# Eight-expert feed-forward block: 39 tiles of 256 rows, or 25 tiles of 256 and 21 units of 128

## The chip, the core and the metric

The kernel runs on one core of a Trainium2 chip. What is measured is the device time of one execution in microseconds (us). The core has five engines with a queue each: TensorE (PE), which loads weights (PEld) and multiplies them with moving columns into PSUM; VectorE (DVE), ScalarE (ACT), GpSimd (POOL) and SyncE (SP). They wait for each other by semaphores.

## What is computed

4096 tokens of 256 channels pass a quaternion rotation, a linear layer, and a top-2-of-8 mixture of experts; then an output layer and the residual. The experts take most of the time.

```python
h = cond(x) @ W_in + b_in                       # x: 8 x 512 tokens, 256 channels
probs = softmax(h @ W_gate + b_gate)
topv, topi = top_k(probs, 2); topv /= sum(topv)
route = zeros_like(probs).at[rows, topi].set(topv)
mid = relu(einsum('nd,edh->neh', h, W1) + b1)    # W1: 8 experts, 256 x 1024
eout = einsum('neh,ehd->ned', mid, W2) + b2      # W2: 8 experts, 1024 x 256
out = x + einsum('ne,ned->nd', route, eout) @ W_out + b_out
```

Only the two chosen experts of a token are computed: 8192 rows in all, sorted by expert.

## The kernel before

**Front part.** x is turned and multiplied, the gate's logits are taken, `z` (the rows that the experts read) is stored to `zbuf` in 16 stores, and VectorE counts the rows of each expert, ranks the experts by count (`order_i`), and gives each row a slot. An expert's rows are padded to a multiple of TS = 256, so NTILE = (8192 + 8*255) // 256 = 39 tiles hold them whatever the counts. Slots become two index tables (`src`, `dst`) through one-hot matrices (L907, L910, L913) and matmuls (L1105). `tile_e` holds each tile's rank.

**Tiles.** Each number is held as a high and a low f16 part, so a product takes three matmuls. Tile a passes through these stages:

- POOL gathers 2 x 128 rows (`gather`, L514), SP turns them with a transposing DMA into `xs` (`turn`, L387).
- PE, first layer (`first_layer`, L1199 to L1201): 4 blocks b of 2 output groups c, each 2 x 3 matmuls of 256 columns: 48 matmuls. The weights lie at `w1_at(e, ...)`, an address made from the rank in a register, so the sequencer does a register operation ("ISA" in the order, FUSED_REGOPS in the trace) for two of three.
- ACT (`tile`, L654): bias, scale and relu of each block into `midf`, two operations of 256 columns.
- DVE (`tile`, L981 and L983): splits each block of 512 columns into high and low f16 (`mids`).
- PE, second layer (`second_layer`, L1229): 48 matmuls of 256 columns. It runs for tile a - 1 after the first layer of tile a.
- DVE (`y_out`, L971) scales the result and adds b2; POOL scatters it to `ybuf` (`scatter`, L522).

**Weights.** An expert's W1 and W2 arrive in f32 (`raw1`, `raw2`, one buffer each; SP, `load_w1` L371, `load_w2` L377), are squared and summed (ACT, L591 and L596; PE, `norms`) and split into f16 parts (ACT and DVE, `piece`; L603 and L793) while the tiles of the rank before run. GT = 4 tiles belong to each rank: phase 0 squares, phase 1 splits W1, phase 2 splits W2, and phase 3 does nothing. PE waits at a rank's first tile for `s_wl`, the count of split pieces. PE's tiles 4 to 27 are a hardware loop; the others are written out.

**End.** The last tile's second layer is done half by half (`last_rows`, L1215); then the pairs of results are loaded, mixed and projected, and the residual (loaded by `load_residual`, bias added in `add_bias`, two per tile from tile 30 on, L998) is added.

## Time and profile before

| | us |
|---|---|
| median of 3 runs (lowest, highest) | 553.31 (551.42, 557.58) |
| time of the profiled execution | 553.89 |
| its span in the trace | 552.1 |
| PE busy | 520.3 (94%) |
| DVE busy | 348.9 (63%) |
| ACT busy | 282.4 (51%) |
| POOL busy | 221.8 (40%) |

The span goes from the first to the last instruction. A matmul's duration in the trace holds its way through the array, which overlaps the next ones; the distance from start to start is what a stream of them costs.

### The profile page before, as it was taken

How to read it: one execution, taken by the hardware profiler on the slowest of the kernel's cores; microseconds unless marked ns; L12 is line 12 of the kernel's file. 1: busy time of each engine (PE TensorE's matmuls, PEld its weight loads, DVE VectorE, ACT ScalarE, POOL GpSimd, SP SyncE). 2: the span in 40 equal slices, each digit the busy share in tenths (PEclk: the TensorE clock that was granted, in tenths of full speed). 3: DMA queues.
4: the chain of work that ended last, by engine and by line, in shares of the span. 5: the costliest groups of instructions: out<-in, count | busy, mean ns of one | idle time of the engine just before them, and what ended most of it. 6: DMA issues, size and time to landing. Idle time of an engine off the chain costs nothing.

```text
span 552.1 us, 13863 instructions
## 1 busy us (share of the span) xinstructions
PE 520.3 (94%) x4337; PEld 450.1 (82%) x4338; DVE 348.9 (63%) x697; ACT 282.4 (51%) x499; POOL 221.8 (40%) x286
## 2 busy tenths in 40 slices
PE   7888966999999999999999999999999999994897
PEld 6555744888888888888888888888888888883786
DVE  4669896686675675665666666675556656651564
ACT  2335782766565565565654654754334324320662
POOL 4400007146373374374375365365334334212132
PEclk8798996999999999999999999999999999998799
DMA  7405445548465364255255256222445445304973
GB/s 210 145 2 165 169 134 161 146 136 171 79 153 162 76 186 128 67 160 163 69 142 170 76 149 166 69 74 78 116 118 143 124 115 137 76 20 142 387 291 134
DMA packets 82312, 74.68 MB, mean 135 GB/s; under 512 B 47511, under 2 KB 70236, under 8 KB 82268
## 3 DMA queue, kind: packets, MB, share of 16 engines
q1 hardware_dynamic: 72336, 49.96, 32.3%
q0 software_dynamic: 8608, 24.13, 14.2%
q8 instruction: 23, 0.38, 0.3%
q10 hardware_dynamic: 1324, 0.05, 0.2%
q14 instruction: 21, 0.17, 0.1%
HBM read 45.53 MB, written 18.61 MB: 116 GB/s over the span
## 4 chain that ended last, share of the span: by engine, by line
PE 85%; DVE 5%; DMA 5%; issue 1%; ACT 1%; SPq 1%; POOL 0%; POOLq 0%; DVEq 0%; ACTq 0%
PE bank L1229 36%; PE bank L1199 13%; PE bank L1200 12%; PE bank L1201 12%; PE bank L1267 5%; DMA z_by_token<-w1s 2%; DVE w1s L822 2%; PE bank L1277 1%; DMA w1s<-y_by_choice 1%; PE bank L1064 1%; DMA w1s<-in_x 1%; PE bank L1215 1%; PE bank L1094 1%; PE bank L1074 1%; DMA region<-z_by_token,src 1%
## 5 line engine op out<-in xcount | busy, mean ns | idle before, releaser
L654 ACT ACTIVATE region<-bank,b1p,cbits 128x256 f32<-128x256 f32 x312 | 159.1, 560 | 183.6 <-PE bank L1201 175.9
L1229 PE MATMUL bank<-w2s,region 128*128 x1824 | 205.3, 273 | 0.1
L1229 PEld LDWEIGHTS bank<-w2s,region 128*128 128x128 f16 x1824 | 178.4, 98 | 21.0 <-issue 0.4
L1199 PE MATMUL bank<-region,w1s 128*128 128x256 f16 x624 | 171.1, 274 | 0.9 <-ACT region L641 0.9
L1200 PE MATMUL bank<-region,w1s 128*128 128x256 f16 x624 | 171.1, 274 | 0.0
L1201 PE MATMUL bank<-region,w1s 128*128 128x256 f16 x624 | 171.0, 274 | 0.0
L522 POOL DMA_INDIRECT y_by_choice<-region,dst x78 | 84.5, 1083 | 189.7 <-DVE region L971 173.2
L514 POOL DMA_INDIRECT region<-z_by_token,src x78 | 77.5, 994 | 86.2 <-DMA z_by_token<-w1s 62.6
L983 DVE TENSOR_TENSOR region<-region 128x512 f16<-128x512 f32 x156 | 108.4, 695 | 5.4
L981 DVE CAST region<-region 128x512 f16<-128x512 f32 x156 | 67.7, 434 | 66.3 <-ACT region L654 61.2
L971 DVE SCALAR_TENSOR_TENSOR region<-bank,cbits,b2b 128x256 f32<-128x256 f32 x76 | 33.3, 479 | 78.4 <-PE bank L1229 77.9
L1199 PEld LDWEIGHTS bank<-region,w1s 128*128 x624 | 62.0, 99 | 8.7 <-issue 1.2
L1201 PEld LDWEIGHTS bank<-region,w1s 128*128 x624 | 61.4, 98 | 7.4
L1200 PEld LDWEIGHTS bank<-region,w1s 128*128 x624 | 61.4, 98 | 7.3
L1094 PE MATMUL bank<-w1s,w2s 128*128 128x256 f32 x128 | 33.3, 404 | 0.0
L1267 PE MATMUL bank<-wout,w2s 128*128 128x256 f32 x120 | 29.9, 394 | 0.0
L1094 PEld LDWEIGHTS bank<-w1s,w2s 128*128 128x128 f32 x128 | 23.8, 196 | 6.6 <-issue 3.8
L1267 PEld LDWEIGHTS bank<-wout,w2s 128*128 128x128 f32 x120 | 22.8, 200 | 2.7
L684 ACT ACTIVATE w2s<-w1s,route 128x256 f32<-128x256 f32 x28 | 12.7, 498 | 18.7 <-DMA w1s<-y_by_choice 18.6
L1277 PE MATMUL bank<-ident,w2s 128*128 128x128 f32 x64 | 10.8, 294 | 10.2 <-DVE w2s L1033 10.2
L603 ACT ACTIVATE w1s<-region,s 128x1024 f16<-128x1024 f32 x16 | 17.6, 1141 | 5.3 <-DVE s L786 5.3
L793 DVE SCALAR_TENSOR_TENSOR w2s<-region,s,w2s 128x1024 f16<-128x1024 f32 x16 | 20.0, 1286 | 0.0
(239 smaller groups left out, 383.3 us busy)
## 6 DMA issues: line engine op xcount, KB each, us to landing
region<-in_L_ffn_W SPq DMA_DIRECT2D x16, 1024.0 KB, 5.2
w1s<-y_by_choice SPq DMA_DIRECT2D x13, 512.0 KB, 10.2
w1s<-in_x SPq DMA_DIRECT2D x8, 512.0 KB, 8.8
z_by_token<-w1s SPq DMA_DIRECT2D x16, 256.0 KB, 2.5
region<-in_x SPq DMA_DIRECT2D x8, 256.0 KB, 4.0
out<-region POOLq DMA_DIRECT2D x8, 256.0 KB, 5.6
region<-z_by_token,src POOLq DMA_INDIRECT x78, 2.9
y_by_choice<-region,dst POOLq DMA_INDIRECT x78
```

What stands on the lines that cost most here:

```text
L514: g.indirect_dma_start(out=gx[:, a % 2, h, :], out_offset=None, in_=zbuf, in_offset=bass.IndirectOffsetOnAxis(ap=at, axis=0)).then_inc(s_g ...
L522: g.indirect_dma_start(out=ybuf, out_offset=bass.IndirectOffsetOnAxis(ap=at, axis=0), in_=ysb[:, a % 2, h, :], in_offset=None).then_inc(s_ ...
L654: m = s.activation(midf[:, b, c * TS:(c + 1) * TS], FB[b][:, c * TS:(c + 1) * TS], ACT.Relu, bias=b1p[:, bass.ds(r, 1), f:f + 1].rearrange ...
L971: last = v.scalar_tensor_tensor(ysb[:, par, h, :], YB[par][:, h * D:(h + 1) * D], cbits[:, 1, 1, bass.ds(r, 1)].bitcast(f32), b2b[:, bass. ...
L981: v.tensor_copy(mids[:, par, 0, b, :], midf[:, b, :]).then_inc(s_mh, 1)
L983: v.tensor_tensor(mids[:, par, 1, b, :], midf[:, b, :], mids[:, par, 0, b, :], ALU.subtract).then_inc(s_mq, 1)
L1094: last = mm(ZB[i % 4][:, t * D:(t + 1) * D], xt_sb[:, i, t, k, :], weff[:, k, :], start=False, stop=(k == KD - 1), skip_group_check=True)
L1199: mm(o, w, xs[:, par, 0, k, :], start=(k == 0), stop=False)
L1200: mm(o, w, xs[:, par, 1, k, :], start=False, stop=False)
L1201: last = mm(o, w1_at(e, 1, k, 2 * b + c), xs[:, par, 0, k, :], start=False, stop=(k == KD - 1))
L1229: last = mm(YB[par][:, h * D:(h + 1) * D], mids[:, par, l, b, c * TS + h * P:c * TS + (h + 1) * P], w2_at(e, w, f), start=(f == 0 and l == ...
L1267: last = mm(bank[2 + par][:, t * D:(t + 1) * D], zt[:, par, t, k, :], wout[:, k, :], start=(k == 0), stop=(k == KD - 1))
```

## The change

25 steps stay tiles of 256 rows. The rows that are left go into 21 units of 128 rows: (8192 + 8*127) // 128 = 71 blocks of 128 rows in all, 50 of them in the tiles. So there are NSTEP = 46 steps, and 71 gathers and scatters in the place of 78. VectorE's planning in the front part is longer: it fills the tiles with each expert's full 256-row blocks, and the rest goes to units. Two units share one buffer of gathered rows and one turn of SP.

A unit's first layer (`first_unit`, in the place of `first_layer`) has 48 matmuls of 128 columns. Its W1 is read from one of two fixed buffers `w1u` (they lie where `raw1` and `raw2` were), into which VectorE copies 4096 f16 values per partition (`copy_w1`), two steps ahead. The second layer (`second_unit`) has 24 matmuls of 256 columns with `w2_at` as before. GT becomes 3, so a rank has no phase 3; the loop on PE takes 6 tiles, three times. The residual's buffers and times move: one `add_bias` per unit from unit 6 on, four after the last `y_out`. `last_rows` is gone.

```diff
-    NTILE = (K * N + E * (TS - 1)) // TS
-    NA = NTILE * H
+    NBIG = -((E * (TS - 1) - K * N) // TS)
+    NUNIT = (K * N + E * (P - 1)) // P - NBIG * H
+    NSTEP = NBIG + NUNIT
+    NTILE = NBIG + (NUNIT + H - 1) // H
+    NA = NBIG * H + NUNIT
...
+        w1u = region[:, RR:RR + 2 * RAW].bitcast(f16).rearrange("p (s l k f) -> p s l k f", s=2, l=2, k=KD)
...
-        GT = NT * P * K // TS // E
+        GT = (NBIG - 1) // E
...
+            count = incl[:, :, NT - 1]
+            link(v.tensor_copy(cnti[:, 0, :], count))
+            v.tensor_scalar(small[:, 0, :], count, float(P - 1), None, ALU.add)
...
+            link(v.scalar_tensor_tensor(small[:, 1, :], cnt[:, 5, :], 0.0, cnt[:, 3, :], ALU.max, ALU.min))
...
+            link(v.tensor_tensor(over, over, bc(small[:, 5, :].unsqueeze(2), [P, E, NT]), ALU.mult))
+            link(v.tensor_tensor(sv[:], sv[:], over, ALU.add))
...
+            def copy_w1(v_):
+
+                u = v_ - NBIG
+                if v_ < NSTEP:
+                    r = dve.value_load(tile_e[0:1, v_:v_ + 1], min_val=0, max_val=E - 1)
+                    if u < 2:
+                        dve.wait_ge(s_wl, 4 * E)
+                    else:
+                        dve.wait_ge(s_mp, 4 * (v_ - 1))
+                    v.tensor_copy(w1u[:, u % 2].rearrange("p l k f -> p (l k f)"),
+                                  w1s[:, bass.ds(r, 1)].rearrange("p e l k f -> p (e l k f)")
+                                  ).then_inc(s_wu[u % 2], 1)
...
+            for a in range(NSTEP):
+                step(a)
+                if a >= NBIG - 2:
+                    copy_w1(a + 2)
+                i = a - NBIG - 2 * H - 2
+                if 0 <= i < NS - NS // 4:
+                    add_bias(i)
+            y_out(NSTEP - 1)
+            for i in range(NS - NS // 4, NS):
+                add_bias(i)
...
+            def first_unit(v):
+
+                u, par = v - NBIG, place(v)[0] % 2
+                rows = slice(place(v)[1] * P, (place(v)[1] + 1) * P)
+                pe.wait_ge(s_xd[par], rows_done(place(v)[0]))
+                pe.wait_ge(s_wu[u % 2], u // 2 + 1)
+                for b in range(4):
+                    pe.wait_ge(s_mf, v * 4 + (b - 3))
+                    for c in range(2):
+                        o = FB[b][:, c * P:(c + 1) * P]
+                        f = slice((2 * b + c) * P, (2 * b + c + 1) * P)
+                        for k in range(KD):
+                            mm(o, w1u[:, u % 2, 0, k, f], xs[:, par, 0, k, rows], start=(k == 0), stop=False)
+                            mm(o, w1u[:, u % 2, 0, k, f], xs[:, par, 1, k, rows], start=False, stop=False)
+                            last = mm(o, w1u[:, u % 2, 1, k, f], xs[:, par, 0, k, rows], start=False,
+                                      stop=(k == KD - 1))
+                    last.then_inc(s_mp, 1)
+
+            def second_unit(v, e):
+
+                pe.wait_ge(s_ys, v - 1)
+                for b in range(4):
+                    pe.wait_ge(s_mq, v * 4 + (b + 1))
+                    for c in range(2):
+                        f = 2 * b + c
                         for l, w in ((0, 0), (1, 0), (0, 1)):
+                            last = mm(YB[v % 2][:, 0:D], midu[:, v % 2, l, b, c * P:(c + 1) * P], w2_at(e, w, f),
                                       start=(f == 0 and l == 0 and w == 0), stop=(f == KF - 1 and w == 1))
+                last.then_inc(s_yp, 1)
...
+            for v in range(NBIG, NSTEP):
+                first_unit(v)
+                if v == NBIG:
+                    second_layer(v - 1, (v - 1) % 2, expert(v - 1))
+                else:
+                    second_unit(v - 1, expert(v - 1))
+            second_unit(NSTEP - 1, expert(NSTEP - 1))
```

On PE, in the kernel before, a group of the first layer in one of the last tiles (`mid_relu` is the semaphore that says ACT has emptied the bank; `w1s` holds all ranks' W1, `region` the turned rows) reads:

```order
L1199 ISA [waits mid_relu]
L1199 MATMUL bank<-region,w1s 128x256
L1200 MATMUL bank<-region,w1s 128x256
L1201 ISA
L1201 MATMUL bank<-region,w1s 128x256
```

In the changed kernel the end of a unit's first layer, and the start of the second layer of the unit before it, read:

```order
L1302 MATMUL bank<-region 128x128
L1334 TENSOR_LOAD tile_e
L1334 ISA x2
L1314 ISA [waits mid_split,y_ready]
L1314 MATMUL bank<-w2s,region 128x256 x2
L1314 ISA
L1314 MATMUL bank<-w2s,region 128x256
```

The first layer's matmuls are 128 columns wide and have lost both the register operations and `w1s` as an operand (the copy lies in `region`); the second layer keeps two register operations for three matmuls, and one read of `tile_e` stands between the two.

On DVE, in the kernel before, the end of tile a's split, `y_out` of tile a - 1 and two `add_bias` read (from tile 30 on):

```order
L981 CAST region<-region 128x512 [waits mid_relu]
L983 TENSOR_TENSOR region<-region 128x512 [waits mid_high]
L966 TENSOR_LOAD tile_e
L966 ISA x2
L971 ISA [waits rows_scattered1,y_product]
L971 SCALAR_TENSOR_TENSOR region<-bank,cbits,b2b 128x256 x2
L998 TENSOR_TENSOR region<-region,boutb 128x512 [waits residual_loaded2] x2
```

In the changed kernel the same place in a unit reads:

```order
L1066 CAST region<-region 128x256 [waits mid_relu]
L1068 TENSOR_TENSOR region<-region 128x256 [waits mid_high]
L1036 TENSOR_LOAD tile_e
L1036 ISA x2
L1042 ISA [waits rows_scattered0,y_product]
L1042 SCALAR_TENSOR_TENSOR region<-bank,cbits,b2b 128x256
L1052 TENSOR_LOAD tile_e
L1052 ISA x2
L1057 ISA [waits mid_product]
L1057 COPY region<-w1s 128x4096
```

The operations are half as wide, and a second read of `tile_e` and the copy stand between one unit's `y_out` and the next unit's split.

## Rows read from the trace of the kernel before

**Rows 1.** Page: each engine's busy time; TensorE's granted clock in 40 slices

```profile
PE 520.3 (94%) x4337; PEld 450.1 (82%) x4338; DVE 348.9 (63%) x697; ACT 282.4 (51%) x499; POOL 221.8 (40%) x286
...
PEclk8798996999999999999999999999999999998799
```

**Rows 2.** Chain that ended last: start us, duration us, what

```profile
112.43 5.24 PE bank L1229 x48
122.91 5.24 PE bank L1229 x48
...
490.83 5.24 PE bank L1229 x48
496.07 5.25 PE bank L1215 x48
```

**Rows 3.** Timeline, 72 to 76 us: start us, duration us, engine, line, operation

```profile
72.39 1.26 PEld L1105 LDWEIGHTS bank<-region 128*128 128x128 f16 x32 [0.88 <-issue]
72.42 1.37 PE L1105 MATMUL bank<-region 128*128 128x78 f16 x32 [0.51 <-DVE region L913]
```

**Rows 4.** Groups by line and shape: count | busy us, mean ns | idle

```profile
L983 DVE TENSOR_TENSOR region<-region 128x512 f16<-128x512 f32 x156 | 108.4, 695 | 5.4
...
L981 DVE CAST region<-region 128x512 f16<-128x512 f32 x156 | 67.7, 434 | 66.3 <-ACT region L654 61.2
...
L971 DVE SCALAR_TENSOR_TENSOR region<-bank,cbits,b2b 128x256 f32<-128x256 f32 x76 | 33.3, 479 | 78.4 <-PE bank L1229 77.9 <-issue 0.4
...
L907 DVE TENSOR_TENSOR region<-iota,slot 128x4096 f16<-128x4096 f16 x2 | 4.6, 2280 | 0.0
...
L910 DVE TENSOR_TENSOR w2s<-iota,slot 128x2496 f16<-128x2496 f16 x2 | 2.9, 1447 | 0.0
```

**Rows 5.** PE's sequencer, L1236, 435 to 440 us: ns min/median/max, first start

```profile
L1236 PEldq TENSOR_LOAD <-tile_e x1: 309/309/309, 436.3 to 436.3; - x1
```

**Rows 6.** L1229, 436 to 440 us: weight loads and the sequencer's register operations

```profile
L1229 PEld LDWEIGHTS bank<-w2s,region x17: 98/98/98, 438.2 to 439.9; 128*128 128x128 f16 x17
...
L1229 PEldq FUSED_REGOPS  x11: 46/46/46, 437.1 to 439.6; - x11
```

**Rows 7.** Timeline of weight loads (PEld), 438 to 439 us

```profile
438.06 0.10 PEld L1201 LDWEIGHTS bank<-region,w1s 128*128 x1
```

**Rows 8.** DVE's sequencer at L966, the whole span

```profile
L966 DVEq TENSOR_LOAD <-tile_e x38: 299/302/791, 103.5 to 492.5; - x38
L966 DVEq FUSED_REGOPS  x38: 190/190/216, 104.3 to 492.8; - x38
```

**Rows 9.** Timeline of ACT, 129 to 139 us

```profile
130.25 3.02 ACT L654 ACTIVATE region<-bank,b1p,cbits 128x256 f32<-128x256 f32 x6 [4.10 <-POOL b1p L507]
...
136.36 1.90 ACT L596 ACTIVATE w2s<-region 128x2048 f16<-128x2048 f32 x1
```

**Rows 10.** Timeline of DVE, 129 to 139 us

```profile
131.30 0.59 DVE L981 CAST region<-region 128x512 f16<-128x512 f32 x1 [2.08 <-ACT region L654]
131.93 0.77 DVE L983 TENSOR_TENSOR region<-region 128x512 f16<-128x512 f32 x1
132.62 0.57 DVE L981 CAST region<-region 128x512 f16<-128x512 f32 x1
```

**Rows 11.** Timeline of DVE, 434 to 436 us

```profile
434.17 1.28 DVE L998 TENSOR_TENSOR region<-region,boutb 128x512 f32<-128x512 f32 x2
```

**Rows 12.** Timeline of SP's queue, 127 to 129.5 us

```profile
127.84 0.41 SPq L377 DMA_DIRECT2D region<-in_L_ffn_W  x1
```

**Rows 13.** Timeline of weight loads (PEld), 127.6 to 128.3 us

```profile
127.55 0.32 PEld L1229 LDWEIGHTS bank<-w2s,region 128*128 128x128 f16 x3
128.00 0.10 PEld L1199 LDWEIGHTS bank<-region,w1s 128*128 x1
```

**Rows 14.** Timeline of DVE, 48 to 64 us

```profile
48.62 0.17 DVE L885 TENSOR_SCALAR cnti<-w2s 128x8 int32<-128x8 f32 x1
...
59.34 0.88 DVE L822 SCALAR_TENSOR_TENSOR w1s<-bank,sx,w1s 128x256 f16<-128x256 f32 x2 [1.52 <-ACT w1s L579]
```

More of the change, by code:

```diff
@@ L135, in moe_program @@
         cnt = sb("cnt", [P, 8, E], f32)
-        cnti = sb("cnti", [P, 2, E], i32)
+        small = sb("small", [P, 6, E], f32)
+        cnti = sb("cnti", [P, 4, E], i32)
         order_i = sb("order_i", [P, E], i32)
@@ L268, in moe_program @@
         s_wh, s_wl = sem("weights_high"), sem("weights_low")
+        s_wu = [sem(f"unit_weights_copied{i}") for i in range(2)]
         s_bsq = sem("b1_squared")
@@ L511, in gather @@
             def gather(a):
-                for h in range(H):
+                for h in range(halves(a)):
                     at = src[:, 1, a * H + h:a * H + h + 1]
@@ L657, in tile @@
                     m.then_inc(s_mf, 1)
-                if j + 1 < E:
-                    if phase(a) == 0:
+                if v < NBIG and j + 1 < E:
+                    if phase(v) == 0:
                         w1_squares(j + 1)
                         w2_squares(j + 1)
-                    if 0 < phase(a) < 3:
+                    if 0 < phase(v) < 3:
                         for i in range(2):
-                            piece(j + 1, 2 * (phase(a) - 1) + i)
-            for a in range(NTILE):
-                tile(a, a % 2, a // GT)
+                            piece(j + 1, 2 * (phase(v) - 1) + i)
+            for v in range(NSTEP):
+                step(v)
             def copy_mix(i, par):
@@ L962, in shares, with y_out @@
                 v.tensor_tensor(route[:, 1, :], route[:, 0, :], mx[:, 2, :], ALU.mult).then_inc(s_rte, 1)
[L964 to L967 removed]
+            def y_out(v_):
+                a, half = place(v_)
+                r = dve.value_load(tile_e[0:1, v_:v_ + 1], min_val=0, max_val=E - 1)
+                dve.wait_ge(s_yp, v_ + 1)
                 if a >= 2:
[L969 to L971 removed]
+                    dve.wait_ge(s_sc[a % 2], a // 2 * (16 * H))
+                for h in range(H) if half is None else (half,):
+                    o = h if half is None else 0
+                    last = v.scalar_tensor_tensor(ysb[:, a % 2, h, :], YB[v_ % 2][:, o * D:(o + 1) * D],
                                                   cbits[:, 1, 1, bass.ds(r, 1)].bitcast(f32),
@@ L990, in tile @@
                 if a:
-                    y_out(a - 1, 1 - par)
+                    y_out(a - 1)
                 else:
```

186 lines of the change are left out of this document (100 added, 86 removed).

## Prediction, made before the changed kernel was run

> **What bounds the kernel now.** I read the page first, for who is busy: PE 94%, DVE 63%, ACT 51%, POOL 40%, and TensorE's granted clock at 0.9 or more of full speed in all slices from the eighth on but two at the end [rows 1]. Then the chain that ended last, for where that time lies. Between 112 and 491 us it shows nothing but PE, one second layer after another [rows 2]: 10.48 us from one to the next (122.91 - 112.43), of which 5.24 is the second layer and so 5.24 the first. Each is 48 matmuls of 256 columns, 5.24 / 48 = 109.2 ns apiece. From the second layer at 112.43 to the one at 490.83 there are 36 steps, 10.51 us on average, so PE hardly ever waits. A tile costs what its 96 matmuls cost, padding included. After the last one (496.07 + 5.25 = 501.3) a chain of evacuation, scatter, loads and the output stage follows, which the change leaves as it is.
>
> **Removed.** 14 of 39 tiles: 14 x 10.48 = 146.7 us of PE.
>
> **Added on PE.** 21 units with 48 matmuls of 128 columns and 24 of 256. The 24 have the form of those in the old second layer, register operations in the same ratio: 24 x 109.2 ns = 2.62 us. No row has 128 f16 columns in a stream. The nearest is L1105, 32 matmuls of 78 columns, each with weights of its own, in a slice with a granted clock of 0.9 or more (the sixth, [rows 1]): the weight loads take 1.26 us from the first start to the last end [rows 3]; one takes 98 ns [rows 6], so they start every (1.26 - 0.098) / 31 = 37.5 ns. Loads thus overlap each other and the matmuls. Between 78 columns at 37.5 and 256 at 109.2 the slope is 0.403 ns a column, which gives 57.6 ns at 128, and 48 x 57.6 = 2.77 us. From below, half of 109.2 (54.6 ns) gives 2.62; from above, loads that did not overlap (98 ns) would give 4.70. I take 57.6, since the row at 78 columns has already shown the faster pace. A unit is then 2.77 + 2.62 = 5.39 us, and 21 of them 113.2 us.
>
> The Trainium skill, "TensorE: Matmul & The Clock Gate", section "Back-to-back issue gap", speaks against this: it gives a sustained ~81 ns per matmul at 128 columns when weight load and matmul alternate. By it a unit would take 6.51 us, and the sum below would be 23.5 us higher. The pace of 37.5 ns in this trace does not agree with it.
>
> **Does PE's sequencer keep up?** The read of `tile_e` starts at 436.3 [rows 5] and the second layer's first register operation is at 437.1 [rows 6]: 0.85 us to its end. The last weight load issued ahead of the read starts at 438.06 [rows 7], so the queue holds about 1.8 us, or 16 matmuls. At 57.6 ns that is 0.92 us, just enough to cover 0.85. One stream at 37.5 ns a pair shows that the sequencer feeds 128-column matmuls at constant addresses. I allow 0.05 us a unit: 1.0 us.
>
> **Added on DVE.** The two-source f16 operation costs 2280 ns for 4096 columns and 1447 for 2496 [rows 4]: 0.52 ns a column and 147 ns fixed. Two operations on f32 input of 512 columns show what one source saves: (434 - 147) / (695 - 147) = 0.52 of the time per column, the cast against the subtraction [rows 4]. Applied to f16, the copy takes 147 + 4096 x 0.27 = 1.26 us. The bound above is the two-source row, 2.28; below nothing is cheaper than the 0.15 fixed. I take 1.26.
>
> DVE's cycle in a unit: blocks of 512 columns start 1.32 us apart when nothing holds them (132.62 - 131.30), where the cast took 0.59 and the subtraction 0.77 [rows 10] in place of 0.434 and 0.695 on average [rows 4]; so 1.09, and less 256 columns of each (0.52 x 256 = 133 for the one, 548 / 2 = 274 ns for the other) 0.68. Four blocks 2.72, `y_out` 0.48 [rows 4], the copy 1.26. A value load is 0.302 + 0.190 [rows 8] and with the next register operation 0.61; it hides behind the operation before it except for 0.18 and 0.13. Sum 4.77 us, under 5.39. In 12 units `add_bias` adds 0.64 (1.28 / 2, [rows 11]): 5.41, level with PE. What DVE falls behind costs nothing at first: a unit's last block is split about 5 us before PE wants it, and a copy is ready some 3 us before its unit. So the copy costs nothing up to about 1.5 us. ACT empties six operations in 3.02 us [rows 9], 0.50 each for 256 columns; at that price, an upper bound, a unit's eight take 4.0 us.
>
> **Three tiles per rank in place of four.** PE at a rank's first tile now follows right after W2's split. The trace has one such place, rank 0 to 1, where no phase 3 lies between: three weight loads start 0.11 us apart from 127.55, and the next, due at 127.88, starts at 128.00 [rows 13], 0.12 us late. Seven boundaries: 0.9 us. W2 of the next rank is asked for at 127.84 [rows 12] and its squares start at 136.36 [rows 9], 8.5 us later, behind other work. The same distance holds at each rank from now on.
>
> **Front part.** The planning on DVE gets 12 more operations. Small ones take 0.17 us [rows 14] plus a wait, three or four on 256 columns about 0.4: 2.9 us together. They stand ahead of the one-hots. Behind them DVE sits idle 1.52 us at 59.34 [rows 14], which takes up half, and four one-hot operations shrink from 2496 to 2272 columns, 4 x 224 x 0.52 ns = 0.5 us. Left 0.9; with the longer rank table I take 1.0. The bounds are 0 and 2.9.
>
> **Sum**, against the profiled execution's 553.9 (span 552.1 and 1.8 around it; the median is 0.6 lower): 553.9 - 146.7 + 113.2 + 1.0 (sequencer) + 0.9 (ranks) + 1.0 (front) = 523.3. I say 523.
>
> **Rivals.**
>
> - DVE becomes the bound (12%). If the copy runs at the two-source pace, 2.28 us, DVE's cycle is 5.79 us and 6.43 with `add_bias`. Some seven units run 0.40 over PE and twelve 1.04: 15.3, less about 2.2 of slack before PE waits for a copy, 13 us: 536. For it: no row shows an f16 copy. Against: the cast's halved slope.
> - The narrow matmuls run slower than interpolated (7%), between 57.6 and 98 ns because each brings a weight load. The middle, 78 ns, gives 48 x 20.4 ns x 21 = 20.6 us more: 544. For it: each pair has a 98 ns load; against: the 37.5 ns. The page of the Trainium skill named above would put the pace near this one.
> - Weights come late (4%). If W2 landed so late at each of seven boundaries that PE waits 2.5 us, the time is 541. Against: the place at 127.84 to 136.36.
> - Slower than before (6%): weight loads of 98 ns do not overlap in the narrow stream. A unit is 4.70 + 2.62 = 7.32 us, and 21 cost 153.7 where 146.7 were removed: 523.3 + 40.5 = 564. It decides from (30.6 / 21 + 2.77) / 48 = 88 ns a matmul on. Against it stands the row at 37.5 ns.
>
> That the change does nothing can't be: the number of steps is fixed in the program.
>
> **How the numbers follow.** The forecast has 68%, its own range 518 to 528 (54.6 ns instead of 57.6 takes 3 us off, no front or sequencer cost 2; the full front cost adds 2, two 0.1 us stalls a unit 4). The rest, 3%, is what I don't see. About 1% is what a measurement of this kernel can tell from no change. The range from 517 to 541 takes in the forecast, the DVE case and late weights (84%), and leaves out the two paces. Faster by over 1% are all cases but the last and a part of the unseen: 91%; slower 6%; within 1% 3%.
>
> **What would show it.** In the changed profile: second layers 10.48 us apart for tiles and about 5.4 for units; starts 57 to 58 ns apart at L1300 to L1302; the copy (L1057) at about 1.26 us; DVE idle behind PE ahead of `y_out` (L1042) in the early units; PE's idle ahead of L1300 small. Copies of over 2 us with PE waiting for DVE would show the first rival; starts of 80 ns or more the paces; idle ahead of L1280 at rank starts the weights. The first tile's first matmul should come about 1 us later than before. Clock slices below 0.9 between tiles and end would refute that 5.4 us units keep PE busy.

## The result, and the profile after

The changed kernel takes 524.81 us (median of 4 runs, 521.84 to 526.88); the kernel before, run beside it, takes 552.37. The ratio is 0.948, with a 95% interval of 0.940 to 0.956: faster. The profiled execution took 526.88 us, with a span of 524.9.

The page of the changed kernel: busy time of each engine, and TensorE's granted clock in 40 slices.

```profile
PE 488.4 (93%) x4505; PEld 424.3 (81%) x4506; DVE 366.8 (70%) x781; ACT 286.6 (55%) x555; POOL 221.9 (42%) x274
...
PEclk8799798799999999999999999999999999996899
```

PE still bounds it: 32 us less of busy time, 93% of the span. DVE went from 63% to 70% [rows 1]. The granted clock is at 0.9 or more from the ninth slice to the end of the units.

**Units, early.** PE's timeline in the changed kernel (start us, duration us, engine, line, operation): the end of one unit's first layer and the second layer of the unit before it.

```profile
401.82 0.22 PE L1300 MATMUL bank<-region 128*128 128x128 f16 x1
401.88 0.22 PE L1301 MATMUL bank<-region 128*128 128x128 f16 x1
401.93 0.22 PE L1302 MATMUL bank<-region 128*128 128x128 f16 x1
401.99 2.78 PE L1314 MATMUL bank<-w2s,region 128*128 x24
```

The first of the first layer's 48 matmuls starts at 399.31 and the last at 401.93: (401.93 - 399.31) / 47 = 55.8 ns apart, though each loads its own weights. That takes 2.68 us, and second layers from 364.89 to 428.49 start 5.30 us apart, twelve times in a row. Nothing holds PE there.

**Units, late.** From the unit at 428.49 on, the starts are 5.67, 5.89, 5.71, 5.80, 5.72, 5.70 and 5.70 us apart. PE's and DVE's timelines around one of these, and the waits of PE's sequencer ahead of the first layers between 428 and 466 us (times, then ns min/median/max, first and last start):

```profile
448.89 0.22 PE L1300 MATMUL bank<-region 128*128 128x128 f16 x1 [0.34 <-issue]
```

```profile
L1295 PEldq EVENT_SEMAPHORE  x7: 1016/1100/1285, 430.3 to 464.8; - x7
```

```profile
448.71 0.68 DVE L1083 TENSOR_TENSOR w2s<-w2s,boutb 128x512 f32<-128x512 f32 x1
449.31 0.28 DVE L1066 CAST region<-region 128x256 f16<-128x256 f32 x1
449.62 0.43 DVE L1068 TENSOR_TENSOR region<-region 128x256 f16<-128x256 f32 x1
...
451.61 0.42 DVE L1068 TENSOR_TENSOR region<-region 128x256 f16<-128x256 f32 x1
452.48 0.48 DVE L1042 SCALAR_TENSOR_TENSOR region<-bank,cbits,b2b 128x256 f32<-128x256 f32 x1 [0.44 <-issue]
453.26 1.24 DVE L1057 COPY region<-w1s 128x4096 f16 x1 [0.29 <-issue]
454.42 0.68 DVE L1083 TENSOR_TENSOR w2s<-w2s,boutb 128x512 f32<-128x512 f32 x1
```

This is a whole DVE cycle, 454.42 - 448.71 = 5.71 us, and DVE waits for no other engine in it. Its only idle time is 0.44 us ahead of `y_out` and 0.29 ahead of the copy, each behind a `value_load`. PE's sequencer stands 1.0 to 1.3 us in a wait ahead of each first layer, and in all seven the wait ends 0.05 us after a copy ends (453.26 + 1.24 = 454.50 and 454.55, for one): the two steps of lead are used up, and PE waits for the copy. DVE is the bound here. The seven steps take 40.19 us where seven at 5.30 take 37.10: 3.1 us.

**Tiles.** The first second layer starts at 106.28 and the 24th at 348.89: 242.6 us. Before, the same 23 steps took 242.2 (101.65 to 343.81). The shorter ranks cost 0.4 us.

**Front part.** That first second layer was at 101.65 before, so 4.6 us were lost ahead of it. PE's timelines, from 44 to 60 us before and from 51 to 66 after:

```profile
44.59 2.82 PE L1094 MATMUL bank<-w1s,w2s 128*128 128x256 f32 x8
...
47.88 2.54 PE L1094 MATMUL bank<-w1s,w2s 128*128 128x256 f32 x8
...
54.83 0.39 PE L1091 MATMUL bank<-w1s,ones 3*128 3x512 bf16 x1
55.15 1.99 PE L1094 MATMUL bank<-w1s,w2s 128*128 128x256 f32 x8
```

```profile
57.33 0.60 PE L1172 MATMUL bank<-w1s,ones 3*128 3x512 bf16 x1 [3.59 <-DVE w1s L873]
57.86 3.78 PE L1175 MATMUL bank<-w1s,w2s 128*128 128x256 f32 x8
61.58 0.60 PE L1172 MATMUL bank<-w1s,ones 3*128 3x512 bf16 x1
62.11 2.71 PE L1175 MATMUL bank<-w1s,w2s 128*128 128x256 f32 x8
64.75 0.38 PE L1172 MATMUL bank<-w1s,ones 3*128 3x512 bf16 x1
```

These are the `z_pair` products of the front part. They are counted from 0, and number 7 needs a PSUM bank that DVE's `z_low(3)` (two operations, for the low f16 part of z) must have read. DVE before, and in the changed kernel:

```profile
53.17 2.44 DVE L822 SCALAR_TENSOR_TENSOR w1s<-bank,sx,w1s 128x256 f16<-128x256 f32 x6
```

```profile
53.67 1.03 DVE L958 TENSOR_TENSOR w2s<-w2s 128x512 f32<-128x512 f32 x1
...
56.40 2.05 DVE L873 SCALAR_TENSOR_TENSOR w1s<-bank,sx,w1s 128x256 f16<-128x256 f32 x5
```

`z_low(3)` now starts at 56.40; before it was at 53.17. Of these 3.23 us the planning's growth is 2.8 (48.74 to 56.40 instead of 48.30 to 53.17); 0.44 lay already ahead of the first `z_pair` (34.94 instead of 34.50). Before, `z_low(3)` had ended 0.8 us ahead of `z_pair(7)`, and, counted from the first `z_pair`, number 7 now starts at 22.39 us instead of 20.33. PE stands 3.59 us there, more than these 2.1, because it came earlier: in the trace of before, `z_pair` 3 and 4 had been slow (2.82 and 2.54 us). Behind the wait the next 16 matmuls take 3.78 and 2.71 us for eight instead of 1.99. The view by windows (stretch: its length, busy time of PE, PEld, DVE, ACT and POOL, then PE's granted clock, DMA share, GB/s) tells why:

```profile
57.90:61.50 3.60, 3.60 (x9) 2.48 (x8) 3.60 (x6) 1.39 (x4) 0.00 (x0) 0.50 0.70 240
60.00:63.00 3.00, 3.00 (x7) 1.64 (x7) 3.00 (x4) 2.89 (x4) 0.00 (x0) 0.50 0.30 103
65.00:69.00 4.00, 4.00 (x18) 2.96 (x17) 4.00 (x4) 3.94 (x7) 0.00 (x0) 1.00 0.39 131
```

The granted clock is 0.50 behind the wait, up to 63.3 us, and 1.00 from 63.6 on. From `z_pair` 7 to 9 it takes 7.42 us instead of 4.48. So the 4.6 us are 0.4 from ahead of the first `z_pair`, about 2.9 from the lower clock, and the rest from the later `z_low(3)`.

The end behind the units is equal: 552.1 - 501.3 before, 524.9 - 474.2 after.

### The profile page after: what moved, and what is told of

The parts are those of the page before. It is cut to its first block, busy times and chain, and to the rows that moved or that the text cites. A ratio compares the mean times of both kernels' runs of the same rounds, so it can differ in the third digit from the quotient of the medians.

```text
span 524.9 us, 14143 instructions
## 1 busy us (share of the span) xinstructions
PE 488.4 (93%) x4505; PEld 424.3 (81%) x4506; DVE 366.8 (70%) x781; ACT 286.6 (55%) x555; POOL 221.9 (42%) x274
## 4 chain that ended last, share of the span: by engine, by line
PE 88%; DVE 4%; DMA 4%; issue 1%; ACT 1%; SPq 1%; POOL 0%; POOLq 0%; DVEq 0%; ACTq 0%
PE bank L1327 25%; PE bank L1314 11%; PE bank L1280 9%; PE bank L1282 8%; PE bank L1281 8%; PE bank L1370 5%; PE bank L1175 4%; PE bank L1300 4%; PE bank L1301 4%; PE bank L1302 4%; PE bank L1380 1%; PE bank L1145 1%; DMA w1s<-in_x 1%; DMA w1s<-y_by_choice 1%; DVE w1s L873 1%
## 5 line engine op out<-in xcount | busy, mean ns | idle before, releaser
L705 ACT ACTIVATE region<-bank,b1p,cbits 128x256 f32<-128x256 f32 (+1 forms) x368 | 162.9, 518 | 151.6 <-PE bank L1282 62.0
L572 POOL DMA_INDIRECT y_by_choice<-region,dst x71 | 86.7, 1222 | 160.2 <-DVE region L1042 148.8
L1327 PE MATMUL bank<-w2s,region 128*128 x1200 | 135.1, 273 | 0.2 <-issue 0.2
L1327 PEld LDWEIGHTS bank<-w2s,region 128*128 128x128 f16 x1200 | 117.0, 98 | 14.3 <-issue 0.6
L1280 PE MATMUL bank<-region,w1s 128*128 128x256 f16 x400 | 109.9, 275 | 0.9 <-ACT region L691 0.9
L1281 PE MATMUL bank<-region,w1s 128*128 128x256 f16 x400 | 109.9, 275 | 0.0
L1068 DVE TENSOR_TENSOR region<-region 128x512 f16<-128x512 f32 (+1 forms) x184 | 105.4, 573 | 6.3
L1282 PE MATMUL bank<-region,w1s 128*128 128x256 f16 x400 | 109.8, 275 | 0.0
L1066 DVE CAST region<-region 128x512 f16<-128x512 f32 (+1 forms) x184 | 70.3, 382 | 48.2 <-ACT region L705 46.1
L1042 DVE SCALAR_TENSOR_TENSOR region<-bank,cbits,b2b 128x256 f32<-128x256 f32 x71 | 32.1, 481 | 48.3 <-PE bank L1327 37.5
L1300 PE MATMUL bank<-region 128*128 128x128 f16 x336 | 57.3, 219 | 2.0 <-issue 2.0
L1314 PE MATMUL bank<-w2s,region 128*128 x504 | 58.5, 273 | 0.0
L1301 PE MATMUL bank<-region 128*128 128x128 f16 x336 | 57.3, 219 | 0.0
L1302 PE MATMUL bank<-region 128*128 128x128 f16 x336 | 57.3, 219 | 0.0
L1314 PEld LDWEIGHTS bank<-w2s,region 128*128 128x128 f16 x504 | 48.3, 98 | 5.5 <-issue 0.3
L1280 PEld LDWEIGHTS bank<-region,w1s 128*128 x400 | 40.0, 100 | 6.9 <-issue 1.5
L1282 PEld LDWEIGHTS bank<-region,w1s 128*128 x400 | 39.4, 99 | 4.9
L1281 PEld LDWEIGHTS bank<-region,w1s 128*128 x400 | 39.4, 99 | 4.5
L1300 PEld LDWEIGHTS bank<-region 128*128 128x128 f16 x336 | 32.8, 98 | 3.9 <-issue 3.7
L1301 PEld LDWEIGHTS bank<-region 128*128 128x128 f16 x336 | 32.9, 98 | 0.1
## 6 DMA issues: line engine op xcount, KB each, us to landing
w1s<-y_by_choice SPq DMA_DIRECT2D x13, 512.0 KB, 10.5
```

Source lines behind the costliest of these rows:

```text
L572: g.indirect_dma_start(out=ybuf, out_offset=bass.IndirectOffsetOnAxis(ap=at, axis=0), in_=ysb[:, a % 2, h, :], in_offset=None).then_inc(s_ ...
L705: m = s.activation(midf[:, b, c * n:(c + 1) * n], FB[b][:, c * n:(c + 1) * n], ACT.Relu, bias=b1p[:, bass.ds(r, 1), f:f + 1].rearrange("p ...
L1068: v.tensor_tensor(mid_at(a, 1, b), midf[:, b, 0:n], mid_at(a, 0, b), ALU.subtract).then_inc(s_mq, 1)
L1280: mm(o, w, xs[:, par, 0, k, :], start=(k == 0), stop=False)
L1281: mm(o, w, xs[:, par, 1, k, :], start=False, stop=False)
L1282: last = mm(o, w1_at(e, 1, k, 2 * b + c), xs[:, par, 0, k, :], start=False, stop=(k == KD - 1))
```

## The experiments

Three groups ran, on three chips, each with the kernel before beside it (the record doesn't say on which chip the comparison above ran): 559.61 us (first group, e1 to e4), 557.02 (second, e5 to e8), 555.86 (third, e9 to e12). The changed kernel took 536.76 and 535.56 us in the last two. So absolute times compare only within a group, and across them the places in the traces do. This table has them, in us: from the first `z_pair` to the first second layer; from there to the 24th second layer (23 tile steps); the last seven steps of the units.

| kernel | front | 23 tile steps | last 7 unit steps |
|---|---|---|---|
| before | 67.15 | 242.2 | |
| changed | 71.34 | 242.6 | 40.19 |
| e1_zlow | 67.94 | 255.8 | 39.34 |
| e2_loads | 70.91 | 251.1 | 37.10 |
| e3_nobias | 71.57 | 251.4 | 37.10 |
| e4_slowcopy | 71.67 | 253.3 | 47.82 |
| e5_again | 71.80 | 250.6 | 40.25 |
| e6_both | 67.74 | 248.5 | 37.13 |
| e7_byreg | 70.96 | 251.1 | 54.36 |
| e8_dose | 71.32 | 246.3 | |
| e9_inplace | 68.64 | 253.3 | 37.80 |
| e10_oneload | 71.42 | 251.4 | 49.08 |
| e11_both | 67.72 | 249.1 | 37.54 |
| e12_again | 71.00 | 247.8 | 39.40 |

### The front part: e1_zlow and e8_dose

```diff
             z_low(2)
+            z_low(3)
...
+            z_low(4)
             link(v.scalar_tensor_tensor(small[:, 1, :], cnt[:, 5, :], 0.0, cnt[:, 3, :], ALU.max, ALU.min))
...
             link(v.tensor_reduce(small[:, 3, :], etmp[:], AX.X, ALU.add))
+            z_low(5)
...
-            for i in range(3, 6):
-                z_low(i)
```

> The changed kernel with three instructions of VectorE moved: the score copies z_low(3), (4) and (5), which stood behind the whole planning of the tiles, stand between its small operations (right behind z_low(2) and at two later places). Nothing is left out. In the changed kernel z_low(3) ended at 56.40 us instead of 53.17, TensorE stood 3.6 us before z_pair(7), the granted clock fell behind that, and the first gather issued at 87.77 instead of 83.14 us. Theory A (TensorE's wait for z_low(3) and the lower clock behind it are the 4.6 us): z_pair(7) starts at 55 us or earlier, the pairs behind it run at 1.99 us for eight matmuls, the first gather issues at 83 to 84 us, and the whole is 3 to 4.6 us shorter than the changed kernel: 520.5 to 522 us. Theory B (the 4.6 us are the longer planning itself, VectorE's or GpSimd's own chain up to the gather): z_pair(7) is early, but the gather still issues near 87 us and the whole stays at 524 to 525 us.

Measured: 532.94 us (528.32 to 533.78), ratio 0.951 (0.943 to 0.960) to before. The median meets neither theory's absolute numbers, since all times of this group are longer. The front part is 67.94 us instead of 71.34. PE's timeline:

```profile
49.70 0.39 PE L1172 MATMUL bank<-w1s,ones 3*128 3x512 bf16 x1
...
51.94 0.38 PE L1172 MATMUL bank<-w1s,ones 3*128 3x512 bf16 x1
52.25 1.99 PE L1175 MATMUL bank<-w1s,w2s 128*128 128x256 f32 x8
```

`z_pair(7)` comes 2.24 us behind `z_pair(6)`, with no wait and at full pace. The planning is as long as in the changed kernel, and the front part is 0.8 us longer than before instead of 4.2. Theory A holds for the place, at 3.4 us. B's chain is the 0.8 that stays. This profiled execution also began its first `z_pair` 3.4 us earlier than the changed kernel's, at 31.52, where nothing was edited, so the front is counted from there; `z_pair(7)` comes 20.42 us later, where it came 22.39 in the changed kernel and 20.33 before.

The reverse, in the kernel before:

```diff
-            link(v.tensor_copy(cnt[:, 3, :], cnti[:, 1, :]))
+            for _ in range(17):
+                link(v.tensor_copy(cnt[:, 3, :], cnti[:, 1, :]))
```

> The kernel before with VectorE's planning made longer and nothing else: one small cast of 0.20 us in it is done 17 times instead of once, 3.2 us more ahead of z_low(3), as the changed kernel's planning is 3.23 us longer. Nothing is left out. Theory A (the front part lost 4.6 us since TensorE waits for z_low(3) and its clock falls behind the wait): z_pair(7) starts near 57.3 us instead of 54.8, the granted clock falls behind it, the first second layer starts near 106 us instead of 101.65, and the whole is 4 to 5 us longer than the kernel before. Theory B (only VectorE's own chain counts, of which 1.52 us of idle time takes up half): about 1.7 us longer. Theory C (the loss came with the changed lists and transfers, not with the planning's length): within 1 us of the kernel before.

Measured: 560.33 us (ten runs, 557.79 to 562.63 and one of 3048.33) against 557.02, ratio 1.0053 (1.0016 to 1.0090). The front part is 71.32 us, 4.2 more than the trace of before has. PE:

```profile
56.40 0.60 PE L1092 MATMUL bank<-w1s,ones 3*128 3x512 bf16 x1 [4.08 <-DVE w1s L822]
56.93 3.78 PE L1095 MATMUL bank<-w1s,w2s 128*128 128x256 f32 x8
...
61.18 2.39 PE L1095 MATMUL bank<-w1s,w2s 128*128 128x256 f32 x8
63.50 0.39 PE L1092 MATMUL bank<-w1s,ones 3*128 3x512 bf16 x1
```

With nothing of the change but the length, the old kernel shows the same kind of wait (4.08 us), the same slow products behind it, and the same front part as the changed one. The dose is some 0.5 us larger than the real growth: `z_pair(7)` comes 22.89 us after the first here. Theory A. In the median 3.3 us arrive, with an interval of 0.9 to 5.0, so the median alone would not tell A from B; the trace does.

### The late units: e2_loads, e3_nobias and e4_slowcopy

```diff
             def step(a):
+                ry = rc = None
+                if a >= NBIG:
+                    ry = dve.value_load(tile_e[0:1, a - 1:a], min_val=0, max_val=E - 1)
+                    if a + 2 < NSTEP:
+                        rc = dve.value_load(tile_e[0:1, a + 2:a + 3], min_val=0, max_val=E - 1)
...
-                    y_out(a - 1)
+                    y_out(a - 1, ry)
...
-                    copy_w1(a + 2)
+                    copy_w1(a + 2, rc)
```

> The changed kernel with VectorE's two value loads of a unit (the expert of y_out and the expert of the W1 copy) issued together at the start of the step, behind the preceding copy of 1.24 us, instead of each directly ahead of the operation that uses it. Nothing is left out. In the changed kernel VectorE stands 0.43 us ahead of y_out and 0.29 us ahead of the copy, and a unit with add_bias takes 5.71 us where TensorE needs 5.30. Theory A (the value loads are exposed because they stand directly ahead of their use, and VectorE bounds the units with add_bias): VectorE's cycle with add_bias falls to about 5.0 us, all 21 units take 5.30 us, and the whole is about 3.1 us shorter than the changed kernel: 521 to 522 us. Theory B (a value load stops VectorE wherever it stands, since it runs only when the instruction before it has ended): the cycle stays at 5.6 to 5.8 us and the whole at 524 to 525 us. Theory C (the units are bounded by something else than VectorE, such as ScalarE's eight activations): the idle time goes, the units keep 5.71 us.

Measured: 532.56 us (527.29 to 534.45), ratio 0.950 (0.941 to 0.959). In the trace the last seven steps take 37.10 us, 5.30 each. DVE's timeline in it:

```profile
441.41 0.42 DVE L1075 TENSOR_TENSOR region<-region 128x256 f16<-128x256 f32 x1
442.58 0.49 DVE L1043 SCALAR_TENSOR_TENSOR region<-bank,cbits,b2b 128x256 f32<-128x256 f32 x1 [0.75 <-PE bank L1322]
442.98 1.22 DVE L1059 COPY region<-w1s 128x4096 f16 x1
444.12 0.69 DVE L1091 TENSOR_TENSOR w1s<-w1s,boutb 128x512 f32<-128x512 f32 x1
```

Now DVE waits for PE ahead of `y_out`, not for its own sequencer, and the copy follows `y_out` without a gap. The loads now stand between the copy (and `add_bias`) of one step and the first cast of the next, and no idle time shows there. Theory A for the place; the median meets neither theory's absolute numbers, here and in the next experiment. A `value_load` costs DVE what does not fit beside the operations ahead of it.

```diff
             def add_bias(i):
+                if i < NS - NS // 4:
+                    v.tensor_tensor(residual(i)[:, 0, 0:1], residual(i)[:, 0, 0:1], boutb[:, 0:1], ALU.add).then_inc(s_xb, 1)
+                    return
```

> The changed kernel with add_bias of the 12 pairs of token tiles that fall inside the units shrunk from 0.68 us to one element each (the output lacks the output bias for these pairs). Theory A (VectorE bounds the units with add_bias: 5.71 us a unit against TensorE's 5.30): all units run at 5.30 us, about 3.1 us off the whole: 521 to 522 us. Theory B (the slower late units come from something else that begins at the same place, such as the transfers of the residuals or a lower clock): the units behind the twelfth stay near 5.7 us and the whole at 524 to 525 us.

Measured: 534.12 us (533.24 to 535.89), ratio 0.957 (0.950 to 0.964). The last seven steps take 37.10 us as well. Theory A: either edit takes DVE's cycle below 5.30, and each gives the whole 3.1 us of this place. The median of the group shows none of it against e1_zlow, which keeps the late loss (39.34 in the trace): what was won here was less than the scatter of the tile steps (251 to 256 us).

```diff
-                    v.tensor_copy(w1u[:, u % 2].rearrange("p l k f -> p (l k f)"),
-                                  w1s[:, bass.ds(r, 1)].rearrange("p e l k f -> p (e l k f)")
+                    src_ = w1s[:, bass.ds(r, 1)].rearrange("p e l k f -> p (e l k f)")
+                    v.tensor_tensor(w1u[:, u % 2].rearrange("p l k f -> p (l k f)"), src_, src_, ALU.max
                                   ).then_inc(s_wu[u % 2], 1)
```

> The changed kernel with the copy of a unit's W1 (4096 columns of half precision, 1.24 us each) written as an operation of two sources, the larger of the tile and itself, which gives the same values. It is a dose of VectorE time in every unit and tests the rival by which the copy's speed decides. Prediction's rival: such a copy takes 2.28 us or more. Theory A (VectorE's chain is the bound once it is over TensorE's 5.30 us): its cycle becomes 4.9 to 5.1 + 1.04 = about 6.0 us without add_bias and 5.71 + 1.04 = 6.75 us with it, so about 12 units at 6.0 and 8 at 6.75: 12 x 0.7 + 8 x 1.04 = 16.7 us longer than the changed kernel, about 541 us. Theory B (two copies ahead of their use are slack enough to take the dose): the units keep 5.30 and 5.71 us, 525 us.

Measured: 553.36 us (550.23 to 557.66), ratio 0.990 (0.986 to 0.994). One group of the trace and one row:

```profile
L1058 DVE TENSOR_TENSOR region<-w1s 128x4096 f16 x21 | 48.4, 2305 | 5.3 <-issue 5.3
```

```profile
412.76 2.31 DVE L1058 TENSOR_TENSOR region<-w1s 128x4096 f16 x1 [0.29 <-issue]
```

The operation takes 2305 ns where the copy takes 1241. Units without `add_bias` start 6.09 to 6.32 us apart where DVE is alone the bound, and those with it 6.77 to 7.03 (expected 6.0 and 6.75). The last seven steps take 47.82 us instead of 40.19, 1.09 more each, for a dose of 1.06: theory A. No unchanged kernel ran in this group; against the 535 to 537 us that it takes in the two others the loss is some 17 us, where 16.7 were expected, but groups differ by several us, and the absolute 541 was missed. This is the rival of the prediction at work: with a two-source copy about three quarters of the gain would be gone (1.0% against 3.5 to 4.0% in the two other groups).

### What the copy buys: e7_byreg, e9_inplace and e10_oneload

```diff
-                pe.wait_ge(s_wu[u % 2], u // 2 + 1)
+                e = expert(v)
...
-                            mm(o, w1u[:, u % 2, 0, k, f], xs[:, par, 0, k, rows], start=(k == 0), stop=False)
-                            mm(o, w1u[:, u % 2, 0, k, f], xs[:, par, 1, k, rows], start=False, stop=False)
-                            last = mm(o, w1u[:, u % 2, 1, k, f], xs[:, par, 0, k, rows], start=False,
+                            w = w1_at(e, 0, k, 2 * b + c)
+                            mm(o, w, xs[:, par, 0, k, rows], start=(k == 0), stop=False)
+                            mm(o, w, xs[:, par, 1, k, rows], start=False, stop=False)
+                            last = mm(o, w1_at(e, 1, k, 2 * b + c), xs[:, par, 0, k, rows], start=False,
...
-                if a >= NBIG - 2:
-                    copy_w1(a + 2)
```

> The changed kernel without the W1 copy: a unit's first layer reads W1 where it lies, at addresses out of a register, as the tiles do, with one value load more on TensorE's queue. Nothing is left out. It prices what the copy buys. Theory A (the sequencer bounds the first layer of a unit: 48 matmuls with weight loads of 37 ns and 32 register operations of 46 ns = 3.25 us instead of 2.68): units of 5.87 us, none bounded by VectorE any more: 21 x 0.57 - 3.1 = about 9 us longer than the changed kernel. Theory B (the sequencer wins back its lag in the second layer, where it needs 24 x 0.037 + 16 x 0.046 = 1.6 us and TensorE 2.62): units of 5.30 us throughout, about 3 us shorter than the changed kernel, and the copy buys nothing. Theory C (a narrow matmul behind a register address costs more than its sequencer time, as the lead is short): units over 6.2 us, 16 us longer or more.

Measured: 577.99 us (575.76 to 583.13), ratio 1.034 (1.028 to 1.041): slower than the kernel before, and 41 us over the changed kernel beside it. Theories A and B are wrong; C ("16 us longer or more") holds, by a wide margin. The weight loads in the trace:

```profile
433.12 0.10 PEld L1298 LDWEIGHTS bank<-region,w1s 128*128 x1 [0.21 <-issue]
433.13 0.10 PEld L1299 LDWEIGHTS bank<-region,w1s 128*128 x1
433.24 0.10 PEld L1300 LDWEIGHTS bank<-region,w1s 128*128 x1
433.37 0.10 PEld L1298 LDWEIGHTS bank<-region,w1s 128*128 x1
...
437.22 0.10 PEld L1300 LDWEIGHTS bank<-region,w1s 128*128 x1
438.15 2.52 PEld L1312 LDWEIGHTS bank<-w2s,region 128*128 128x128 f16 x24 [0.83 <-issue]
440.92 0.10 PEld L1298 LDWEIGHTS bank<-region,w1s 128*128 x1 [0.25 <-issue]
```

Three matmuls with two register addresses take 0.25 us, 16 of them 4.2 us with the gaps between blocks (433.12 to 437.32), where the sum of constant issue and register operations gave 3.25 and constant addresses take 2.68. The `value_load` before the second layer shows as 0.83 us of idle, and the next one as 0.25. A unit takes 7.76 us. The sequencer's own rows tell why (ns min/median/max, first and last start): register operations of a unit's first layer, 433 to 434 us, and of its second layer, 438 to 440.1 us, and the reads of `tile_e`, 430 to 445 us.

```profile
L1298 PEldq FUSED_REGOPS  x4: 46/46/46, 433.0 to 433.8; - x4
...
L1312 PEldq FUSED_REGOPS  x16: 46/46/46, 438.1 to 440.1; - x16
...
L1332 PEldq TENSOR_LOAD <-tile_e x3: 299/301/303, 432.4 to 440.2; - x3
```

A register operation is 46 ns long, but in both layers one starts only every 0.12 to 0.13 us (two of them in each triple of 0.25). The 48 of a unit make up some 6.0 us of the 7.76, and two value loads, 0.65 us each from a read's start (440.18) to the next instruction's (440.82), most of the rest. What theory A had wrong is the 46 ns.

Constant addresses in the same place (against e7_byreg):

```diff
-                e = expert(v)
+                e = E - 1
                 for b in range(4):
```

> The changed kernel without the W1 copy, a unit's first layer reading W1 where it lies, but always that of the last expert, at constant addresses (the units' first layers so use a wrong expert's W1). It tells the address from the place: reading in place with addresses from a register, the units took 7.76 us each instead of 5.30. Theory A (the register addresses cost it: a triple of matmuls took 0.248 us there, of which the sequencer's two register operations alone are 0.092): 5.30 us for every unit, also those with add_bias, since VectorE has no copy to do: about 3 us shorter than the changed kernel on the same chip. Theory B (the place costs it: W1 in its own region is read while other engines write there or transfers land there): units over 6.5 us.

Measured: 533.33 us (2 runs, 530.44 and 536.22), ratio 0.960 (0.955 to 0.965), and the changed kernel in the group 535.56. Most units are 5.30 us apart, the last six among them, between 5.30 and 5.33, with `add_bias`. Theory A: the address costs it, not the place. This kernel also has one `value_load` less per unit than e7_byreg; the next experiment gives that 0.75 us of the 2.46, with register addresses kept. The copy is worth its 1.24 us of DVE because it turns a register address into a constant one.

The front part of this kernel, edited nowhere, tells one thing more. `z_pair(7)` comes 22.44 us after the first, as in the changed kernel. But the slow products lie ahead of the wait here, as they did before the change (2.83 and 2.53 us at `z_pair` 3 and 4); PE waits 2.03 us, no lower clock follows, and the front part is 68.64 us. Against 71.34 that is some 2.7 us for the clock behind the wait; against 67.15, some 1.5 us for the later `z_low(3)` itself. Each of the three is a single trace.

Again against e7_byreg:

```diff
-                e = expert(v)
...
+            was = expert(NBIG - 1)
             for v in range(NBIG, NSTEP):
-                first_unit(v)
+                now = expert(v)
+                first_unit(v, now)
...
-                    second_unit(v - 1, expert(v - 1))
+                    second_unit(v - 1, was)
+                was = now
```

> The version that reads W1 in place at addresses from a register, with one value load on TensorE's queue for each unit instead of two (the expert of the unit before is kept). Nothing is left out. Theory A (TensorE's sequencer bounds these units through and through, at 7.76 us): taking away one value load (0.302 us, 0.151 and 0.018 us of register operations and the check) shortens every unit by 0.45 to 0.6 us, to about 7.25 us, 10 us off the whole. Theory B (the value load waits for the matmuls ahead of it to end and so costs the whole 0.83 us of idle time seen before the second layer): 6.9 us. Theory C (something else bounds these units): 7.7 us.

Measured: 566.58 us (2 runs), ratio 1.020 (1.016 to 1.024); the last seven steps take 49.08 us, 7.01 each. The edit takes 0.75 us off a unit: more than A's 0.45 to 0.6 and a little less than B's 0.83. Not all of it is the `value_load`. The second layer's register operations are of another kind in this program, and closer together:

```profile
L1311 PEldq ALU_OP  x16: 32/32/32, 444.6 to 446.4; - x16
```

From the first of them to the next read of `tile_e` it takes 2.00 us (444.58 to 446.58) instead of 2.12 (438.05 to 440.18). The `value_load` itself is the other 0.65, again more than its own rows add up to (0.47). Nor does it wait for the matmuls ahead of it: in e7_byreg one starts at 437.30, while the last matmul before it runs from 437.23 to 437.46. So theory A holds in kind, with a price that was too low. TensorE's sequencer bounds these units through and through.

### The changed kernel again, and both edits together: e5_again, e6_both, e11_both, e12_again

> The changed kernel unchanged, as the reference for the three kernels beside it on the same chip. In the four experiments before, the kernel before took 559.6 us where it had taken 552.4, and the 24 tiles of 256 rows, which had run almost without a stop (from 106.28 to 348.89 us), took 251 to 256 us, with ScalarE standing still up to 3.7 us at a time. Theory A (that is the chip and not the edits): this kernel shows it too if this is such a chip, at about 529 to 531 us against 559 for before; on a chip like the first it is 524 to 526 against 552. Theory B (the edits cost the tiles 9 to 13 us): no such stops here.

> The changed kernel with both edits at once: z_low(3), (4), (5) inside the planning and the two value loads of a unit at the start of its step. Nothing is left out. Theory A (two separate places, both on the path): the first second layer starts 3.4 us earlier counted from the first z_pair (67.9 instead of 71.3 us), every unit takes 5.30 us (3.1 us in the units with add_bias), so 6.5 us less than the unchanged changed kernel beside it. Theory B (what is won in the front part is lost again later, at the transfers of the first tiles): 3.1 us less or under.

Measured in the second group: e5_again 536.76 us (531.12 to 538.06), ratio 0.960 (0.952 to 0.968); e6_both 526.24 us (525.60 to 527.52), ratio 0.944 (0.938 to 0.949).

> The changed kernel with z_low(3), (4), (5) inside the planning and the two value loads at the start of the step, once more, beside the unchanged one. Nothing is left out. Theory A (two places, 3.4 us in front and 3.1 us in the units): 6.5 us less than the changed kernel beside it. On the chip of the last group it was 10.6 us less (526.2 to 536.8), of which 2 us were shorter stops in the tiles. If those stops are chance, the difference here lies at 6 to 7 us; if the edits shorten them as well, at 9 us or more.

> The changed kernel unchanged, beside the version before it in this group. 524 to 526 us where the kernel before takes 552 (ratio 0.948), 530 to 537 where it takes 557 or more (ratio 0.95 to 0.96).

Measured in the third: e11_both 526.11 us (525.58 to 527.88), ratio 0.947 (0.945 to 0.949); e12_again 535.56 us (531.45 to 539.19), ratio 0.965 (0.960 to 0.969).

Both edits together give the front part of 67.7 us and units of 5.30 us in both groups, so theory A of e6_both holds for the two places, worth 3.3 to 4.1 and 1.9 to 3.1 us in these four traces. The medians differ by 10.5 and 9.4 us, more than the 6.5 of the two places; the spans of the profiled executions by 10.3 (523.5 to 533.8) and 7.0 (525.9 to 532.9). In those traces most of the rest lies in single steps that took longer: of the first pair's 10.3 us, 2.1 in the tiles; of the second's 7.0, 2.6 in the early units, while its tiles went 1.2 the other way. Whether the edits have a part in it has not been settled. The version with both is faster than either kernel. e5_again lies above the 529 to 531 us expected for such a group, and e12_again's ratio above both expected ranges.

In these groups the tile steps take 246 to 256 us instead of 242, in the changed kernel itself (250.6) and in the lengthened old one (246.3) too, so the edits aren't the cause: theory A of e5_again as far as that goes. That it is the chip was not tested. A row group of DVE's casts in the tiles (what the engine sat idle for ahead of them: us, times) of the changed kernel in the first comparison, and of e12_again:

```profile
L1066 DVE CAST region<-region x96: 419/427/605, 104.2 to 350.2; 128x512 f16<-128x512 f32 x96
...
  ACT region L705: 40.9, 51
```

```profile
L1066 DVE CAST region<-region x95: 416/427/607, 103.8 to 352.9; 128x512 f16<-128x512 f32 x95
...
  ACT region L705: 40.6, 27
  issue: 16.7, 12
```

DVE pauses twelve times, up to 2.1 us at once, for nothing that the trace shows ("issue"); ACT stands 6.9 us in eight stops that the view calls "remote". PE feels it at the ranks' starts, where no phase 3 lies any more between W2's split and the next rank:

```profile
133.80 0.28 PE L1280 MATMUL bank<-region,w1s 128*128 128x256 f16 x1 [0.97 <-DVE w2s L844]
```

The boundary at 128 us that cost 0.12 us [rows 13] costs 0.97 here. Three such stops sum to 3.7 us in e12_again. The cause of the pauses stays open.

## Why the prediction came out right, step by step

The forecast was 523 us; the time is 524.81 in the median and 526.88 in the profiled execution, 3.6 over the sum of 523.3, which was made against a profiled execution. By its terms:

- **Removed, 146.7.** Tiles still start 10.48 us apart. Right.
- **Units, 21 x 5.39 = 113.2.** The interpolated pace was 57.6 ns, the measured one 55.8; a unit takes 5.30 us, 1.9 us less in all. The rival with 78 ns, and the Trainium skill's ~81 ns ("TensorE: Matmul & The Clock Gate", "Back-to-back issue gap"), do not hold in this kernel; the row of 78 columns at 37.5 ns [rows 3] told the right thing.
- **Sequencer, +1.0.** With constant addresses nothing was lost in the early units: 0. That the queue just covers one `value_load` agrees with it, and e7_byreg shows what comes when it doesn't.
- **DVE in the units, 0.** The copy was sized at 1.26 us and takes 1.24. The failed term is "it hides behind the operation before it except for 0.18 and 0.13": 0.44 and 0.29 us show in the trace, 0.42 more. So the cycle with `add_bias` is 5.71 instead of 5.41, while PE came out at 5.30 instead of 5.39. The two would have been level and are 0.4 us apart, 3.1 us over the last seven steps. The slack of the steps ahead carries the first ones with `add_bias`, as the prediction said, but not all twelve. e2_loads and e3_nobias each remove these 3.1 us.
- **Ranks, +0.9.** 0.4 in the profiled comparison. In the later groups these boundaries cost more, so the place was the right one to name.
- **Front, +1.0 (0 to 2.9).** Measured +4.6, above its bound; 4.2 of it counted from the first `z_pair`. That the planning grows by 2.9 us was right (2.8). The failed step is "Behind them DVE sits idle 1.52 us at 59.34 [rows 14], which takes up half". It followed DVE's own chain only. It did not ask who waits for the operation that the new ones stand ahead of: `z_low(3)` frees the bank of PE's `z_pair(7)`, and before the change it ended only 0.8 us ahead of that use. PE waits, and its clock is lower behind the wait, a term that the sum doesn't have at all. e1_zlow takes this part away and leaves 0.8 us, near the 1.0 of the prediction; e8_dose makes it appear in the old kernel; e9_inplace, where the clock stays up behind the wait, has 1.5 us left.

The front's miss of 3.6 us is as large as the whole difference of the sum; the other misses nearly cancel (-1.9 - 1.0 - 0.5 + 3.1), and that is luck. The forecast is right because its large terms are (what is removed, and the units' pace), and because the two terms that failed were small beside them. None of the rivals came: e4_slowcopy shows that the first of them was near, one kind of operation away.

## What to carry to other kernels

When operations are put into an engine's queue, look for the next operation behind them that frees a buffer of the bounding engine, and compare the added time with the spare time between that release and its use; a chain's own idle time says nothing of it. Where many narrow matmuls follow one another, a copy to a fixed place can be worth far more than its time, as it takes register addresses out of the stream. Where an engine's own cycle is the bound, a `value_load` belongs behind a long operation of the cycle, not directly ahead of its use.

## What the runs showed of the hardware

- Pairs of weight load and matmul, 128 columns in f16 at constant addresses, start 55.8 ns apart for 48 in a row at a granted clock of 1.00, though one load takes 98 ns.
- With two register addresses for three such matmuls, three take 0.25 us, 83 ns each. The sequencer starts a register operation every 0.12 to 0.13 us there, though each is 46 ns long (e7_byreg).
- On DVE, a `value_load` directly ahead of its use left 0.44 us of idle behind an operation of 0.42 us, and 0.29 behind one of 0.48; two of them behind the copy of 1.22 and `add_bias` of 0.69 us left none. On TensorE's sequencer, where that is the bound, one takes 0.65 us.
- Behind a wait of 3.59 us the granted clock was 0.50 from 57.4 to 63.3 us, the lower of its two levels (1.2 GHz), and then rose to 1.00 (2.4 GHz). A wait did not always do this. Eight traces with a wait of the same kind before `z_pair(7)` have slow products behind it, and so has e8_dose; e9_inplace, with a wait of 2.03 us, has none. The wait of 1.87 us ahead of `z_pair(3)` was followed by slow products in before, e1_zlow and e9_inplace, and by products at full pace in the changed kernel.
- In the three later groups engines paused, up to 6.0 us at once (ACT in e8_dose), at places where the first comparison shows no pause. The changed kernel's gain was 5.2% in that comparison, and 4.0 and 3.5% in the two groups that have it.
